# Decoder layer: the first pair of heads of each batch weighed in float32, with four buffers for the exponentials

## What is computed

```python
qkv = _bitlinear(x, w_qkv).reshape(B, N, 3, H, D)
q, k, v = (qkv[:, :, 0], qkv[:, :, 1], qkv[:, :, 2])
attn = jnp.einsum('bnhd,bmhd->bhnm', q, k) * SCALE
attn = jnp.where(causal, attn, NEG)
attn = jax.nn.softmax(attn, axis=-1)
out = jnp.einsum('bhnm,bmhd->bnhd', attn, v).reshape(B, N, C)
return _bitlinear(out, w_proj)
```

## Time and profile before

| | us |
|---|---|
| median of three runs | 1578.74 |
| the profiled execution | 1573.84 |
| its span | 1572.0 |
| TensorE busy | 1479.5 |
| VectorE busy | 1155.0 |
| GpSimd busy | 962.1 |
| ScalarE busy | 713.9 |

### The profile page before, as it was taken

How to read it: one execution, slowest core, us unless ns; L and a number is a source line. 1 busy time by engine, 2 the same in 40 slices (tenths; PEclk the granted TensorE clock), 3 DMA queues, 4 the chain that set the end, 5 groups by cost and what they waited for, 6 DMA issues and landing times.

```text
span 1572.0 us, 24053 instructions
## 1 busy us (share of the span) xinstructions
PE 1479.5 (94%) x9049; PEld 838.9 (53%) x9049; DVE 1155.0 (73%) x1805; ACT 713.9 (45%) x1252; POOL 962.1 (61%) x704
## 2 busy tenths in 40 slices
PE   2599999999976989999999999999999999999998
PEld 2477888788753434444444444444444444444443
DVE  5789999999856889986776667676677666767511
ACT  4589999999882114223223223222322322322241
POOL 2389999999893328865455445554545544555232
PEclk9799999999997999999999999999999999999999
DMA  3555656555415111112000200110200020010000
GB/s 137 151 135 131 165 147 169 141 148 146 117 59 167 40 40 48 48 54 61 20 21 20 60 28 21 47 34 14 61 21 21 21 61 28 21 34 1 2 26 27
DMA packets 58707, 105.78 MB, mean 67 GB/s; under 512 B 7624, under 2 KB 11872, under 8 KB 58592
## 3 DMA queue, kind: packets, MB, share of 16 engines
q1 hardware_dynamic: 58400, 104.10, 23.7%
q10 hardware_dynamic: 192, 0.14, 0.1%
HBM read 50.74 MB, written 19.92 MB: 45 GB/s over the span
## 4 chain that ended last, share of the span: by engine, by line
PE 70%; DVE 10%; ACT 7%; POOL 6%; issue 5%; DMA 1%; SPq 1%; POOLq 0%; DVEq 0%; ACTq 0%
PE gu L685 20%; PE gu L699 10%; PE y L650 10%; PE y L653 3%; PE y L658 3%; PE y L657 3%; PE y L654 3%; PE gu L636 3%; PE y L656 3%; POOL pL L1471 2%; PE gu L650 2%; DVE blockmax L814 2%; DVE o_sb L854 1%; ACT pH L1212 1%; DVE qkt L794 1%
## 5 line engine op out<-in xcount | busy, mean ns | idle before, releaser
L1568 POOL TENSOR_TENSOR fuL<-fu,fuH 128x512 f16<-128x512 f32 x96 | 126.1, 1313 | 204.2 <-ACT fuH L1372 204.2
L1471 POOL TENSOR_TENSOR pL<-pT,pH 128x768 f16<-128x768 f32 x128 | 216.5, 1693 | 11.0 <-ACT pH L1212 4.8
L650 PE MATMUL y<-kv,toep 128*128 128x512 f32 x424 | 204.1, 599 | 4.1 <-DVE kv L980 2.1
L1013 DVE TENSOR_REDUCE oT<-z 128x64 f32<-128x512 f32 x256 | 175.7, 686 | 8.8
L685 PE MATMUL gu<-fT,wg 128*128 128x512 f16 x768 | 181.4, 379 | 0.3 <-ACT fT L1395 0.3
L685 PE MATMUL gu<-fT,wu 128*128 128x512 f16 x768 | 181.4, 379 | 0.0
L1007 DVE TENSOR_TENSOR y<-y,shared 128x512 f32<-128x512 f32 x108 | 75.3, 697 | 143.4 <-PE y L658 74.1
L1009 DVE TENSOR_TENSOR z<-y,cT 128x512 f32<-128x512 f32 x236 | 162.2, 687 | 19.2 <-PE y L650 15.5
L1372 ACT ACTIVATE fuH<-fu 128x512 f16<-128x512 f32 x96 | 60.2, 627 | 206.3 <-DVE fu L1028 206.3
L699 PE MATMUL gu<-wd,fuH 128*128 128x512 f16 x384 | 145.5, 379 | 0.0
L699 PE MATMUL gu<-wd,fuL 128*128 128x512 f16 x384 | 145.5, 379 | 0.0
(11 more groups left out here) (190 smaller groups left out, 3390.0 us busy)
## 6 DMA issues: line engine op xcount, KB each, us to landing
pack<-qkhl SPq DMA_DIRECT2D x256, 128.0 KB, 2.4
x_sb<-in_x SPq DMA_DIRECT2D x16, 512.0 KB, 4.4
c_sb<-in_ctx SPq DMA_DIRECT2D x32, 256.0 KB, 3.6
hankel<-in_L_xattn_k SPq DMA_DIRECT2D x32, 256.0 KB, 3.6
x_grp<-x_scratch SPq DMA_DIRECT2D x32, 256.0 KB, 3.9
out_y<-yo SPq DMA_DIRECT2D x32, 256.0 KB, 2.8
x_scratch<-x_sb SPq DMA_DIRECT2D x15, 512.0 KB, 2.8
wraw<-in_L_attn_w_qkv SPq DMA_DIRECT2D x3, 1024.0 KB, 9.7
```

The lines of the kernel that those rows point to most:

```text
L650: made = T.matmul(to, tap(h, lb - kb), keys_values(h, kb, half), start=kb == 0, stop=kb == lb)
L1013: V.tensor_reduce(out=oT[h % 2][:, lb, own].rearrange("p (b j) -> p b j", b=HB), in_=z[n % 2][:], op=ALU.add, axis=AXIS.X).then_inc(m_z, 1)
L1471: G.tensor_tensor(pL[n % 2][:], pT[n % NP][:], pH[n % NP][:], ALU.subtract).then_inc(low_done, 1)
L1568: G.tensor_tensor(fuL[:, ib, :], fu[n % 2][:], fuH[:, ib, :], ALU.subtract).then_inc(f_fl, 1)
```

## The change

`W_HEADS` = 2 heads, pair 0 of each batch, are no longer split. `weigh` multiplies `pT` itself with a float32 copy of v, `vW` (32 columns and a column of ones), in six products instead of twelve. Their high and low parts are not made. `split_v` writes `vW` beside a narrower `vHL`, the adding of parts leaves the two heads out, `weighed` copies 33 of 65 columns for them. `pT` has four buffers instead of three; an exponential waits for the low part of pair n - 4, or, where that is a pair 0, for its weighing. `n_split` counts the pairs that are still split. The count of constants that are waited for goes from 21 to 24.

```diff
     PIECES = 2 * CB * INNER // PIECE
-    NX, NPACK, NP = 8, 3, 3
-    HIGH_ON_ACT = (1, 2, 3, 4, 5, 6, 7)
+    NX, NPACK, NP, NPT = 8, 3, 3, 4
+    W_HEADS = 2
     with ExitStack() as ctx:
...
         fw_out = q("fw_out", [P, PIECE], F16)
-        vHL = [q(f"vHL{i}", [P, NT, HEADS, VW + D], F16) for i in range(3)]
+        vHL = [q(f"vHL{i}", [P, NT, HEADS - W_HEADS, VW + D], F16) for i in range(3)]
+        vW = [q(f"vW{i}", [P, NT, W_HEADS, VW], F32) for i in range(3)]
         blockmax = [q(f"blockmax{i}", [P, PAIRS, 6], F32) for i in range(2)]
...
         nmT = [q(f"nmT{i}", [P, N], BF16) for i in range(2)]
-        pT = [q(f"pT{i}", [P, 6, P], F32) for i in range(3)]
+        pT = [q(f"pT{i}", [P, 6, P], F32) for i in range(NPT)]
         pH = [q(f"pH{i}", [P, 6, P], F16) for i in range(3)]
...
         st_pe, exp_done = signal("st_pe"), signal("exp")
-        high_act, high_dve, low_done = signal("p_high_act"), signal("p_high_dve"), signal("p_low")
+        high_done, low_done = signal("p_high"), signal("p_low")
+        v_whole = signal("v_whole")
         pv_pe, pv_out = signal("pv_pe"), signal("pv_out")
...
         wq8 = wq8_dram.rearrange("m n p c -> m (n p c)").rearrange("m (n p c) -> m n p c", p=P, c=PIECE)
-        def high_done(n):
-            b, p = divmod(n, PAIRS)
-            if p in HIGH_ON_ACT:
-                return high_act, b * len(HIGH_ON_ACT) + HIGH_ON_ACT.index(p) + 1
-            other = [i for i in range(PAIRS) if i not in HIGH_ON_ACT]
-            return high_dve, b * len(other) + other.index(p) + 1
+
+        def whole(n):
+            return n % PAIRS == 0
+
+        def n_split(n):
+
+            return n - n // PAIRS
         def wT_ready(w, i):
...
                 b, p = divmod(n, PAIRS)
-                ph, pl, v = pH[n % NP], pL[n % 2], vHL[b % 3]
+                ph, pl = pH[n % NP], pL[n_split(n) % 2]
                 acc = pv[:, 0:NT * 2 * (VW + D)].rearrange("p (t h w) -> p t h w", t=NT, h=2)
-                w.wait_ge(*high_done(n))
-                w.wait_ge(low_done, n + 1)
-                w.wait_ge(v_high, 2 * b + 2)
-                w.wait_ge(v_low, 2 * b + 2)
+                if whole(n):
+                    w.wait_ge(exp_done, n + 1)
+                    w.wait_ge(v_whole, 2 * b + 2)
+                else:
+                    w.wait_ge(high_done, n_split(n))
+                    w.wait_ge(low_done, n_split(n))
+                    w.wait_ge(v_high, 2 * b + 2)
+                    w.wait_ge(v_low, 2 * b + 2)
                 w.wait_ge(const_done, C_ONCE)
...
                             block, h = 2 * hh + t if mt == t else 4 + hh, 2 * p + hh
-                            T.matmul(acc[:, t, hh, :], ph[:, block, :], v[:, mt, h, :], start=mt == 0, stop=False)
-                            made = T.matmul(acc[:, t, hh, :], pl[:, block, :], v[:, mt, h, :], start=False, stop=mt == t)
+                            if whole(n):
+                                made = T.matmul(acc[:, t, hh, 0:VW], pT[n % NPT][:, block, :], vW[b % 3][:, mt, h, :],
+                                                start=mt == 0, stop=mt == t)
+                                continue
+                            v = vHL[b % 3][:, mt, h - W_HEADS, :]
+                            T.matmul(acc[:, t, hh, :], ph[:, block, :], v, start=mt == 0, stop=False)
+                            made = T.matmul(acc[:, t, hh, :], pl[:, block, :], v, start=False, stop=mt == t)
                 made.then_inc(pv_pe, 1)
...
                     w.wait_ge(pv_pe, PAIRS * (b - 2))
-                V.tensor_scalar(vHL[b % 3][:, t, :, 0:D], bank[:].rearrange("p (h d) -> p h d", h=HEADS),
-                                small[b % 4][:, 12 + t:13 + t], None, ALU.mult).then_inc(v_high, 1)
+                v, vhl = bank[:].rearrange("p (h d) -> p h d", h=HEADS), vHL[b % 3][:, t]
+                scale = small[b % 4][:, 12 + t:13 + t]
+                V.tensor_scalar(vhl[:, :, 0:D], v[:, W_HEADS:, :], scale, None, ALU.mult).then_inc(v_high, 1)
+                V.tensor_scalar(vW[b % 3][:, t, :, 0:D], v[:, 0:W_HEADS, :], scale, None, ALU.mult).then_inc(v_whole, 1)
                 w.wait_ge(v_high, n + 1)
-                V.scalar_tensor_tensor(out=vHL[b % 3][:, t, :, VW:VW + D], in0=bank[:].rearrange("p (h d) -> p h d", h=HEADS),
-                                       scalar=small[b % 4][:, 12 + t:13 + t], in1=vHL[b % 3][:, t, :, 0:D],
+                V.scalar_tensor_tensor(out=vhl[:, :, VW:VW + D], in0=v[:, W_HEADS:, :], scalar=scale, in1=vhl[:, :, 0:D],
                                        op0=ALU.mult, op1=ALU.subtract).then_inc(v_low, 1)
...
                 V.tensor_tensor(nt[32:64, :], bank[0:32, 0:N], nt[0:32, :], ALU.subtract).then_inc(mT_low, 1)
-            def high_part(n):
-                w.wait_ge(exp_done, n + 1)
-                if n >= NP:
-                    w.wait_ge(pv_pe, n - NP + 1)
-                V.tensor_copy(pH[n % NP][:], pT[n % NP][:]).then_inc(high_dve, 1)
-
             def finish(b, k):
...
                     V.reciprocal(rl, raw[:, :, :, D])
-                    chain.step(V.tensor_tensor(raw[:, 0, :, 0:D], raw[:, 0, :, 0:D], raw[:, 0, :, VW:VW + D], ALU.add))
+                    raw = raw[:, 0, W_HEADS:, :]
+                    chain.step(V.tensor_tensor(raw[:, :, 0:D], raw[:, :, 0:D], raw[:, :, VW:VW + D], ALU.add))
                 elif k == 1:
...
                         low_max(use)
-                if (n := pair(t, HIGH)) is not None and n % PAIRS not in HIGH_ON_ACT:
-                    high_part(n)
                 for b, k in batches(t, FINISH, 14):
...
                 w.wait_ge(score_scale_done, 1)
-                if n >= NP:
-                    w.wait_ge(low_done, n - NP + 1)
-                S.activation(pT[n % NP][:], s_kq[:, 0:6, :], ACT.Exp, scale=ws[:, 4:5]).then_inc(exp_done, 1)
+                if n >= NPT and whole(n - NPT):
+                    w.wait_ge(pv_pe, n - NPT + 1)
+                elif n >= NPT:
+                    w.wait_ge(low_done, n_split(n - NPT))
+                S.activation(pT[n % NPT][:], s_kq[:, 0:6, :], ACT.Exp, scale=ws[:, 4:5]).then_inc(exp_done, 1)
             def high_part(n):
...
                     w.wait_ge(pv_pe, n - NP + 1)
-                S.activation(pH[n % NP][:], pT[n % NP][:], ACT.Copy).then_inc(high_act, 1)
+                S.activation(pH[n % NP][:], pT[n % NPT][:], ACT.Copy).then_inc(high_done, 1)
             def weighed(n):
...
                     w.wait_ge(o_mult, b - 1)
-                S.activation(oraw[b % 2][:, :, 2 * p:2 * p + 2, :], acc, ACT.Copy).then_inc(pv_out, 1)
+                width = VW if whole(n) else VW + D
+                S.activation(oraw[b % 2][:, :, 2 * p:2 * p + 2, 0:width], acc[:, :, :, 0:width], ACT.Copy).then_inc(pv_out, 1)
             def finish(b, k):
...
                     exponentials(n)
-                if (n := pair(t, HIGH)) is not None and n % PAIRS in HIGH_ON_ACT:
+                if (n := pair(t, HIGH)) is not None and not whole(n):
                     high_part(n)
...
             def low_part(n):
-                w.wait_ge(*high_done(n))
-                if n >= 2:
-                    w.wait_ge(pv_pe, n - 1)
-                G.tensor_tensor(pL[n % 2][:], pT[n % NP][:], pH[n % NP][:], ALU.subtract).then_inc(low_done, 1)
+                w.wait_ge(high_done, n_split(n))
+                if n_split(n) > 2:
+                    w.wait_ge(pv_pe, n - 2 if whole(n - 1) or whole(n - 2) else n - 1)
+                G.tensor_tensor(pL[n_split(n) % 2][:], pT[n % NPT][:], pH[n % NP][:], ALU.subtract).then_inc(low_done, 1)
             def sum_parts(b):
-                raw = oraw[b % 2]
+                raw = oraw[b % 2][:, 1, W_HEADS:, :]
                 w.wait_ge(pv_out, PAIRS * (b + 1))
-                G.tensor_tensor(raw[:, 1, :, 0:D], raw[:, 1, :, 0:D], raw[:, 1, :, VW:VW + D], ALU.add).then_inc(o_sum, 1)
+                G.tensor_tensor(raw[:, :, 0:D], raw[:, :, 0:D], raw[:, :, VW:VW + D], ALU.add).then_inc(o_sum, 1)
             def add_piece(n):
...
                 G.memset(vHL[i][:, :, :, D:VW], 1.0).then_inc(const_done, 1)
+                G.memset(vW[i][:, :, :, D:VW], 1.0).then_inc(const_done, 1)
             for t in STEPS:
-                if (n := pair(t, LOW)) is not None:
+                if (n := pair(t, LOW)) is not None and not whole(n):
                     low_part(n)
```

More of the change, by code:

```diff
@@ L226, in decoder_kernel @@
         const_done = signal("const_done")
-        C_IDENT, C_BASE, C_PART1, C_ONCE = 2, 7, 16, 21
+        C_IDENT, C_BASE, C_PART1, C_ONCE = 2, 7, 16, 24
         rows_in = signal("rows_in")
```

## The result

The changed kernel takes 1578.05 us in the median of 22 runs (1576.37 to 1580.06), the kernel before 1574.3 in the median of 22 (1573.05 to 1579.07). The ratio is 1.0015, interval 1.0008 to 1.0022: +2.4 us, from 1.3 to 3.5. The direction is the one forecast and the time lies in the range, but by this ratio the change costs half of what was said. The base was off as well: the median of three runs, 1578.74, stood over 4 us above the median of 22.

What follows compares the result with a forecast made beforehand. A chain of waits over TensorE, ScalarE and VectorE was taken to set the 24.80 us period. Terms +8.2, +1.6, +0.1 and -3.3 gave +6.6 us, 1580.4 or 1585.3 by base; forecast 1584, range 1573 to 1591.

Steps and rivals of the forecast that it cites:

- The price of the weighing: TensorE, pair 0 of each batch: twelve float32 instructions at 112 ns, 1.34 us for 0.36, +0.98 us a batch.
- The other end, no overlap of load and stream: Rival, TensorE's weighing: 140 ns an instruction, +1.32 us a batch, total +10.7, 1589 us; chance 0.12.
- Its way into the period: From pair 0's weighing through TensorE's scores to pair 5's exponential on ScalarE: +0.79 us a period.
- The closing over `spread_c`: Loop's end: the delay passes ScalarE's quotient step and VectorE's low part of V to TensorE's scale spreading; period +0.82 with V's split.
- batches 3 to 12 run at the steady period: +8.2: Steady stretch: ten batches, each 0.82 us longer.
- Batches 1 and 2 (+1.6) and batch 0 (+0.1): Start: batches 1 and 2 wait for TensorE in the same way; batch 0 has idle time behind its weighing.
- The tail, -3.3: Batches 13 to 15: GpSimd's saved low part counts, less the longer weighing; 0.8, 0.8 and 1.7 us, ends 0 and -5.6.
- GpSimd's relief, 0 in the steady stretch: GpSimd saves 1.86 us a batch, but nobody waits for it in the steady stretch, so 0 there.
- The fourth buffer, 0: ScalarE's exponentials: the extra buffer removes a wait that the steady stretch doesn't show, so 0.
- The idle time: Rival: TensorE's 0.9 us idle a period absorbs the product, period 24.8 to 24.9, about -2 in all, 1577 us; chance 0.24.
- GpSimd's relief doesn't win: Rival denied here: GpSimd's full queue stretches its neighbours, so relieving it makes the kernel faster, 1573 us; chance 0.14.
- The base: Time before to which +6.6 was added: profiled execution 1573.84 us (giving 1580.4) or three-run median 1578.74 (giving 1585.3).

Runs made afterwards that it cites:

- e3_price: The changed kernel with pair 0's high and low parts still made, though nobody multiplies them: +0.32% on the kernel before.
- e4_relief: The changed kernel with pair 0's exponentials and V in float16, so TensorE pays nothing: period 25.05 us against 24.80 in the kernel before.
- e11_last: The kernel before with four exponential buffers and pair 0 whole in float32 only in batches 13 to 15: 1570.76 us, ratio 0.9959 to before.
- e1_buffers: The kernel before with the fourth exponential buffer and nothing else: ratio 0.9995 to before, period 24.79 us.
- e10_relief_hold: e4_relief plus a GpSimd wait: q and k's rest is made only after VectorE's division. 0.57% faster than before by the ratio, period 24.62 us.
- e13_before_hold: The kernel before plus a GpSimd wait: q and k's rest is made only after VectorE's division. Ratio 1.0002 to before, period 24.79 us.
- e8_six: The kernel before with six float16 products for pair 0 instead of twelve, all parts still made: period 24.80 us.

## Why the forecast was half right

- **The price of the weighing: right.** Twelve instructions, 112 ns each by the row of `spread_c`, measured 111.7. The sum missed the first load, which hides under earlier work: +0.90 in place of +0.98. The other end, no overlap of load and stream, fell. It fell because an instruction of 33 columns costs the same 112 ns as one of 128, so the stream is hidden. The Trainium skill ("TensorE: Matmul & The Clock Gate", The mechanism) lets a load overlap running products only for another row group; the equal 112 ns disagree.
- **Its way into the period: right in kind, smaller.** From exponential 48 to that of pair 5 it is 0.67 us longer, forecast 0.79; 0.08 of the difference is that first load. The closing over `spread_c` was wrong: `blockmax` of pair 7 closes it, and +0.69 arrives, not 0.82.
- **The failed step is the sum's term "batches 3 to 12 run at the steady period: +8.2".** It measured +6.25. 1.3 us of the 1.95 is the period, 0.82 against 0.69. The other 0.65 is that before didn't run at 24.80 throughout: its batches 3 and 7 take 25.01 and 25.11 and batch 12 takes 24.04, against 25.50, 25.48 and 24.61 after. I multiplied a difference by ten where three of the base's ten batches had another length.
- **Batches 1 and 2 (+1.6) and batch 0 (+0.1).** Measured +0.06, +0.59 and +0.43. So this term is mis-sized too, by 0.6 us in all. Batch 1 had room for nearly all of the price (`e3_price`, +0.06). Batch 0's +0.43 isn't the price: `e3_price` has -0.05 there and `e4_relief`, which pays none, +0.42. Why a relieved batch 0 is longer wasn't looked into.
- **The tail, -3.3: the number right**, -3.31, in part by luck. `e11_last` shows the same gain by itself. But the working had it all from GpSimd's relief, and of the 3.8 us up to the last exponential `e3_price` has 2.2 without it, 1.2 of them as in `e1_buffers`, with the clock's fall in the last batch before among the causes.
- **GpSimd's relief, 0 in the steady stretch: right here, but the reason given is incomplete.** `e3_price` and the change have the same period. That "nobody waits for GpSimd" holds in the waits, yet a GpSimd that runs ahead changes which of two engines starts first, and `e4_relief` loses 0.25 us a period by it.
- **The fourth buffer, 0:** right alone, but 1.3% in the combination, which the change has. The prediction gave only the first.
- **The rivals.** The idle time didn't take the price (period 25.49, not 24.8 to 24.9). GpSimd's relief doesn't win.
- **The base.** I put 1584 between 1580.4 and 1585.3, from a median of three. With 22 runs at 1574.3 my +6.6 would have been 1581, +0.42%, against the interval's upper end of +0.22%. So the base isn't the excuse: the size was off, +4.0 for +6.6 by the traces. The rest, from +4.0 to the ratio's +2.4, fits the lower clock of some executions of the kernel before.

## What to carry to other kernels

A cost that repeats with the period is paid in every batch, a relief is earned only where its engine is waited for: look for the stretch where that is so and change only it (here the last three batches: 0.9959 in place of 1.0015; by the spans 3.2 us under the kernel before in place of 2.7 over it). Put TensorE's granted clock beside every stretch and every execution that is compared. Before multiplying a difference by the number of periods, read every period of the kernel before. And where work is taken from GpSimd, look at what VectorE runs beside it: who starts first may turn round.

## What the runs showed of the hardware

VectorE and GpSimd instructions with two inputs in SBUF hold each other up, and the one that starts first wins. VectorE's division and GpSimd's instructions around it, before:

```profile
244.83 1.65 POOL L1471 TENSOR_TENSOR pL<-pT,pH 128x768 f16<-128x768 f32 x1
...
246.06 1.51 DVE L854 TENSOR_TENSOR o_sb<-oraw,osmall 128x1024 f32<-128x1024 f32 x1
...
246.44 2.15 POOL L1464 TENSOR_TENSOR qkhl<-qkt,qkhl 128x512 f16<-128x512 f32 x1
```

After:

```profile
247.79 1.16 POOL L1473 TENSOR_TENSOR qkhl<-qkt,qkhl 128x512 f16<-128x512 f32 x1
...
248.09 1.95 DVE L862 TENSOR_TENSOR o_sb<-oraw,osmall 128x1024 f32<-128x1024 f32 x1
...
249.22 2.32 POOL L1480 TENSOR_TENSOR pL<-pT,pH 128x768 f16<-128x768 f32 x1 [0.27 <-ACT pH L1220]
```

`e4_relief`:

```profile
246.30 1.16 POOL L1477 TENSOR_TENSOR qkhl<-qkt,qkhl 128x512 f16<-128x512 f32 x1
...
246.48 2.07 DVE L865 TENSOR_TENSOR o_sb<-oraw,osmall 128x1024 f32<-128x1024 f32 x1
...
247.42 2.62 POOL L1484 TENSOR_TENSOR pL<-pT,pH 128x768 f16<-128x768 f32 x1
```

`e10_relief_hold`:

```profile
245.09 1.22 DVE L865 TENSOR_TENSOR o_sb<-oraw,osmall 128x1024 f32<-128x1024 f32 x1
...
246.39 1.16 POOL L1477 TENSOR_TENSOR qkhl<-qkt,qkhl 128x512 f16<-128x512 f32 x1 [1.44 <-DVE o_sb L865]
247.51 1.65 POOL L1484 TENSOR_TENSOR pL<-pT,pH 128x768 f16<-128x768 f32 x1
```

`e13_before_hold`:

```profile
244.82 1.66 POOL L1471 TENSOR_TENSOR pL<-pT,pH 128x768 f16<-128x768 f32 x1
...
245.75 1.81 DVE L854 TENSOR_TENSOR o_sb<-oraw,osmall 128x1024 f32<-128x1024 f32 x1
```

`e10_relief_hold` has each alone: the division 1.22, q and k's rest 1.16, a low part 1.65 us. Now count the time for which an instruction of GpSimd that started earlier still runs beside the division: 0.42 us before (to 246.48), 0.73 in `e13_before_hold`, 0.86 after, 0.98 in `e4_relief`. The division is 0.29, 0.59, 0.73 and 0.85 longer: each time the overlap less 0.13 to 0.14. The other way round, GpSimd's instruction that starts into the division overlaps it by 1.13 (before), 0.82 (after) and 1.13 (`e4_relief`), and is 0.99, 0.67 and 0.97 longer: the overlap less 0.14 to 0.16. So the later one makes next to no progress until the earlier ends. VectorE's row maximum, which reads the scores from PSUM, isn't touched: the one at 245.21 before lies wholly beside the low part of 244.83 and takes 0.94 us, the group's mean after is 0.95. The Trainium skill ("SBUF — State Buffer", Who interferes with whom) has the rule: a VectorE instruction with two inputs in SBUF contends with a GpSimd instruction that reads SBUF. The rows agree, and with them a case that the forecast should have weighed.

The adding of parts turned round in the same way: before, VectorE's began at 243.19, 0.16 us ahead of GpSimd's, and took 0.75 us to its 1.53; after, GpSimd's began at 244.43, 0.28 ahead, and took 0.97 to VectorE's 1.17.

GpSimd's share of 99% was in part this, not work: q and k's rest took 1.40 us in the mean before and takes 1.16 after the change.

What stays open: what holds the period of the kernel before at 24.80. Less on TensorE (`e8_six`) doesn't move it, nor does a division up to 0.15 us longer; less on GpSimd and VectorE, kept apart, brings 24.62. Open too is what makes TensorE's clock fall in one kernel's batch 13 or 15 and not in another's with nearly the same work, and how much of the 29.3 to 31.6 us from the last exponential to the second part it explains: `e4_relief` needs 30.7 at a clock like that of before.
